# Ten gather slots instead of five, and round loops unrolled by two, in a two-layer graph network

## What is computed

```python
h = relu(layernorm(x))
# layer 0, the edge network: one message per edge
z   = concat([h[src], edge_attr]) @ W1 + b1          # 96 -> 64
m   = silu(silu(layernorm(z, g1, be1)) @ W2 + b2)    # 64 -> 64
agg = segment_sum(m, dst)
x   = x + layernorm(silu(concat([agg, h]) @ Wu + bu), gn, bn)
h = relu(layernorm(x))
# layer 1
agg = segment_sum(h[src], dst)
x   = x + (relu((h + agg) @ M1 + c1) @ M2 + c2)
```

## Time and profile before

| what | value |
|---|---|
| median of 3 runs | 7667.49 us (7646.55 to 7680.56) |
| profiled execution, whole | 7691.83 us |
| its span, first to last instruction | 7690.1 us |
| setup / edge network / update / layer 1 / last product, from | 0 / 209 / 5522 / 5870 / 7480 us |
| busy: PE, POOL, DVE, ACT | 5612.1, 4279.3, 3146.2, 2092.2 us |
| TensorE clock, mean of the span | 0.607 of full |

### The profile page before, as it was taken

The page is one execution under the profiler, slowest core; times in us unless marked ns, Lnnn a source line. Parts: engine busy times, 40 slices in busy tenths (PEclk is TensorE's granted clock), DMA queues, the critical chain, the costliest instruction groups (busy, mean ns, idle before and its releaser), DMA issues. The chain is left out here.

```text
span 7690.1 us, 119604 instructions
## 1 busy us (share of the span) xinstructions
PE 5612.1 (73%) x32337; PEld 4448.0 (58%) x32337; DVE 3146.2 (41%) x12654; ACT 2092.2 (27%) x4111; POOL 4279.3 (56%) x4223
## 2 busy tenths in 40 slices
PE   6577676776767676776767676767757888888879
PEld 5455555555555555555555555555646777777776
DVE  6333333333333333333333333333365565555651
ACT  1111111111111111111111111111135555555551
POOL 3655555555555555555555555555436666666651
PEclk9555555555555555555555555555558999999995
DMA  2111111111111111111111111111111000000001
GB/s 82 33 30 30 29 29 29 29 29 29 29 29 29 29 30 29 29 29 29 29 29 29 28 29 29 30 29 29 25 38 20 17 17 17 17 18 17 17 14 34
DMA packets 281547, 216.06 MB, mean 28 GB/s; under 512 B 152958, under 2 KB 213403, under 8 KB 280985
## 3 DMA queue, kind: packets, MB, share of 16 engines
q0 software_dynamic: 134304, 137.82, 10.1%
q1 hardware_dynamic: 147193, 77.59, 3.8%
HBM read 200.56 MB, written 14.40 MB: 28 GB/s over the span
## 5 line engine op out<-in xcount | busy, mean ns | idle before, releaser
L733 POOL DMA_INDIRECT gat<-layer_rows,idx x4025 | 4049.9, 1006 | 2929.1 <-ACT idx L791 1786.1
L770 PE MATMUL ps<-oh,edge_buffers 128*64 128x64 f32 x6250 | 874.2, 317 | 699.7 <-issue 485.1
L741 PE MATMUL ps<-w1e,edge_buffers 64*128 64x128 f32 (+1 forms) x3750 | 1136.4, 443 | 164.6 <-issue 142.7
L1497 ACT ACTIVATE node_buffers<-ps 125x800 bf16<-125x800 f32 x1152 | 947.5, 838 | 764.7 <-PE ps L1548 565.3
L770 PEld LDWEIGHTS ps<-oh,edge_buffers 128*64 128x64 f32 x6250 | 730.9, 221 | 726.2 <-issue 448.1
L741 PEld LDWEIGHTS ps<-w1e,edge_buffers 64*128 64x128 f32 (+1 forms) x3750 | 924.5, 319 | 332.6 <-issue 313.7
L749 PE MATMUL ps<-ident,edge_buffers 128*128 128x128 f32 x1875 | 563.6, 439 | 701.0 <-DVE edge_buffers L993 616.9
L922 ACT ACTIVATE edge_buffers<-ps,gcol 128x384 f32<-128x384 f32 x625 | 415.3, 665 | 1954.7 <-remote 1822.9
L797 DVE TENSOR_TENSOR cT<-cT,ps 64x64 f32 x805 | 170.8, 212 | 1881.1 <-remote 1339.0
L965 DVE TENSOR_TENSOR edge_buffers<-ps,gat 128x320 f32<-128x320 f32 x625 | 306.1, 490 | 1520.7 <-remote 1239.5
L1548 PE MATMUL ps<-node_buffers 128*128 128x200 bf16 x4608 | 646.8, 265 | 333.9 <-ACT node_buffers L1497 218.2
(11 more groups left out here) (187 smaller groups left out, 4812.6 us busy)
## 6 DMA issues: line engine op xcount, KB each, us to landing
gat<-layer_rows,idx POOLq DMA_INDIRECT x4025
edge_buffers<-in_edge_pairs SPq DMA_DIRECT2D x625, 64.0 KB
edge_buffers<-in_edge_last SPq DMA_DIRECT2D x625, 16.0 KB
node_buffers<-in_x SPq DMA_DIRECT2D x5, 625.0 KB
layer_rows<-node_buffers SPq DMA_DIRECT2D x25, 125.0 KB
residual_rows<-node_buffers SPq DMA_DIRECT2D x5, 625.0 KB
layer_rows<-node_buffers SPq DMA_DIRECT2D x5, 625.0 KB
node_buffers<-residual_rows POOLq DMA_DIRECT2D x25, 125.0 KB, 4.5
```

Of the source, the lines that this page charges most:

```text
L733: pool.indirect_dma_start(out=gat[:, j, c, :], out_offset=None, in_=table[:, :], in_offset=bass.IndirectOffsetOnAxis(ap=idx[:, j, c:c + 1] ...
L741: mm = pe.matmul(zp[j % 2][:, 2 * k * F:(2 * k + 1 + two) * F], ea[0:(1 + two) * ED, j, k * 128:(k + 1) * 128], w1e[0:(1 + two) * ED, 0:(1 ...
L770: mm = pe.matmul(to[j % 2][0:F, 0:WIN], rows_of[:, c, :], oh[:, j, c, :], start=(c == 0), stop=(c == BC - 1))
L1497: a.activation(cnt[0:TP, s, ch * 8 * T:(ch + 1) * 8 * T].rearrange("p (b k) -> p b k", b=2), built[ch % 2][0:TP, :, :], ACT.Copy).then_inc ...
```

## The change

1. **Ten slots.** Gathered rows and row numbers of the edge network get two sets of five slots each, `deep[0..1]` and `deep_idx[0..1]`, in memory that another stage uses otherwise. An even round uses set 0, an odd round set 1. There are ten completion semaphores in place of five. POOL's step for block n now waits for the row add of block n-10, and ACT writes the row numbers of block n+10 behind the squares of block n (ten sets ahead of the first step).
2. **Rounds unrolled by two.** Which set a step uses must be known when the code is written, so the loop body is now two rounds (ten steps), 60 passes; two rounds stand ahead of it on every engine, three behind it. All other buffers keep five slots.
3. **Semaphores.** To free five, the setup shares some: the two loads that DVE's offsets wait for count on one, and a few steps of one engine count on a semaphore that this engine already has. The order of the instructions stays the same.
4. Layer 1 keeps `idx` and `gat`; its counts start at 63 rounds in place of 125, since set 0 has taken the even rounds only.

```diff
+        again(XB)
+        deep = [view([128, UN, BC, F]) for _ in range(2)]
+        deep_idx = [view([128, UN, BC], i32) for _ in range(2)]
...
-                    v.wait_ge(s_dst, 16)
-                    v.wait_ge(s_head, 16)
+                    v.wait_ge(s_dst, 32)
...
-        def rounds(eng, step, lag, lead=1):
+        def rounds(eng, step, lag):
+            assert ROUNDS % 2 == 1
 
-            for j in range(lead * UN):
-                step(j // UN, j % UN)
-            with eng.Fori(lead, ROUNDS - 1) as r:
-                for j in range(UN):
-                    step(r, j)
-            for j in range(UN + lag):
-                step(ROUNDS - 1, j)
+            for j in range(2 * UN):
+                step(j // UN, j % UN, j // UN)
+            with eng.Fori(1, (ROUNDS - 3) // 2) as e:
+                for j in range(2 * UN):
+                    step(2 * e + j // UN, j % UN, j // UN)
+            for j in range(3 * UN):
+                step(ROUNDS - 3 + j // UN, j % UN, j // UN % 2)
+            for j in range(UN, UN + lag):
+                step(ROUNDS - 1, j, 0)
...
-        g_gat = [sem(f"rows_gathered{j}") for j in range(UN)]
+        g_gat = [[sem(f"l0_rows_gathered{p}_{j}") for j in range(UN)] for p in range(2)]
...
                     wait(pool, g_idx, n + 1)
 
-                    wait(pool, g_z, n - UN + 1)
+                    wait(pool, g_z, n - 2 * UN + 1)
                     wait_alone(pool, "gpsimd")
-                    gather(pool, ptab, n, j, g_gat[j])
+                    gather(pool, ptab, j, g_gat[p][j], deep[p], deep_idx[p])
...
-                        if there(n + UN):
-                            indices(a, n + UN, s).then_inc(g_idx, 1)
+                        if there(n + 2 * UN):
+                            indices(a, n + 2 * UN, s, deep_idx[p]).then_inc(g_idx, 1)
...
-                    for j in range(UN):
-                        indices(a, j, j).then_inc(g_idx, 1)
-                    rounds(a, step, 4, lead=2)
+                    for j in range(2 * UN):
+                        indices(a, j, j % UN, deep_idx[j // UN]).then_inc(g_idx, 1)
+                    rounds(a, step, 4)
...
-                        wait(v, g_gat[s], q * (16 * BC) + 16 * BC)
+                        half = q // 2 if isinstance(q, int) else q >> 1
+                        wait(v, g_gat[p][s], half * (16 * BC) + 16 * BC)
...
-                                        gat[:, s, :, :], ALU.add).then_inc(g_z, 1)
+                                        deep[p][:, s, :, :], ALU.add).then_inc(g_z, 1)
...
-        L0_ROWS = ROUNDS * 16 * BC
+        L0_ROWS = (ROUNDS + 1) // 2 * 16 * BC
```

More of the change, by code:

```diff
@@ L602, in _ @@
                 v.tensor_reduce(worst[:, 5:6], worst[:, 0:5], X, ALU.max).then_inc(s_test, 1)
[L603 to L605 removed]
+                v.wait_ge(s_tot, 3)
+                v.tensor_copy(off_i[:, :], ag[1][:, 0:NT]).then_inc(s_hk, 1)
+                v.wait_ge(s_tot, 4)
                 v.tensor_reduce(worst_row[:, :], ag[0][0:1, 0:128], X, ALU.max).then_inc(s_test, 1)
@@ L722, in _, with gather @@
                 pe.matmul(zp[0][:, 0:3 * F], ones[:, :], rows[:, 2:5, :].rearrange("o k f -> o (k f)"),
-                          start=True, stop=True).then_inc(s_bp, 1)
-                pe.wait_ge(s_deg, 3)
+                          start=True, stop=True).then_inc(s_tot, 1)
+                pe.wait_ge(s_hk, 8 + HEAD)
                 pe.matmul(ag[1][:, 0:NT], onesm[0:NT, :], carry[:, :], start=False, stop=True).then_inc(s_tot, 1)
                 pe.wait_ge(s_test, 10)
-                pe.transpose(ag[0][0:1, 0:128], worst[:, 5:6], ident[:, :]).then_inc(s_wt, 1)
-        def gather(pool, table, n, j, done):
+                pe.transpose(ag[0][0:1, 0:128], worst[:, 5:6], ident[:, :]).then_inc(s_tot, 1)
+        def gather(pool, table, j, done, to=gat, at=idx):
             for c in range(BC):
                 pool.indirect_dma_start(
-                    out=gat[:, j, c, :], out_offset=None, in_=table[:, :],
-                    in_offset=bass.IndirectOffsetOnAxis(ap=idx[:, j, c:c + 1], axis=0)).then_inc(done, 16)
+                    out=to[:, j, c, :], out_offset=None, in_=table[:, :],
+                    in_offset=bass.IndirectOffsetOnAxis(ap=at[:, j, c:c + 1], axis=0)).then_inc(done, 16)
         def edge_products(pe, j):
@@ L787, in load_edges, with indices @@
             sp.dma_start(ea[0:ED, j, (BC // 2) * 128:], of(edge_last)).then_inc(done, 16)
-        def indices(a, n, j):
-            return a.activation(idx[:, j, :], block_of(src_all, n), ACT.Copy)
+        def indices(a, n, j, to=idx):
+            return a.activation(to[:, j, :], block_of(src_all, n), ACT.Copy)
         def add_sums(v, n, j, of=ag):
@@ L850, in _, with step @@
             def _(sp):
-                def step(r, j):
+                def step(r, j, p):
                     n = r * UN + j
@@ L902, in _, with step @@
                     edge_products(pe, 0).then_inc(g_ep, 1)
-                    rounds(pe, step, 5, lead=2)
+                    rounds(pe, step, 5)
             @block.scalar
             def _(a):
-                def step(r, j):
+                def step(r, j, p):
                     _, s, n = lagged(r, j, 0)
@@ L997, in _ @@
                 with v.If(flagged(v) == 0):
-                    rounds(v, step, 6, lead=2)
+                    rounds(v, step, 6)
         def general(layer, table):
@@ L1023, in gpsimd @@
                     wait_alone(pool, "gpsimd")
-                    gather(pool, table, n, 0, x_gat)
+                    gather(pool, table, 0, x_gat)
             def scalar(a):
@@ L1467, in step @@
                     wait_alone(pool, "gpsimd")
-                    gather(pool, htab, n, j, g_gat[j])
+                    gather(pool, htab, j, g_gat[0][j])
                 def both(r):
@@ L1513, in sums @@
                     n = r * UN + j
-                    wait(pe, g_gat[j], r * (16 * BC) + L0_ROWS + 16 * BC)
+                    wait(pe, g_gat[0][j], r * (16 * BC) + L0_ROWS + 16 * BC)
                     wait(pe, k_oh, n + 1)
```

33 lines of the change are left out of this document (14 added, 19 removed).

## The result

The changed kernel took 7773.28 us (median of 4 runs, 7747.21 to 7815.74) against 7662.44 us for the kernel before beside it: a ratio of 1.0149, interval 1.0089 to 1.021. The forecast was 7685 us, +0.2%. Twelve more runs in another set gave a median of 7756.34 us against 7656.83. So the change is slower both times, by 1.4 and 1.3% in the medians, and the sign is surer than the size.

The account below looks back on a forecast made before the run. PE's signals arriving late while POOL issues gathers without a break were taken to bound the edge network. 7691.8 + 31.3 - 13.3 = 7709.8 us profiled, 24.3 above the median, so 7685 us (+0.2%); range 7550 to 7810.

Parts of the forecast that it names:

- the likeliest case: Whole kernel: start and end terms within their bounds plus the spread of runs, 7640 to 7715 us; chance 0.55.
- rival C: POOL's stream: free slots let two-block runs grow to three, 8.72 us a block, 156 us slower, 7840 us; chance 0.14.
- Rival D: DVE's loop: code fetched again each pass, 85 to 170 us slower, 7770 to 7855 us; chance 0.07.
- What bounds the kernel now: Edge network: PE's signals reach others late while POOL issues gathers without a break; 8.46 us a block.
- Ten slots, steady state: 0 us: Edge network's steady part: each row add still frees one block of gathers, so 8.46 us a block stays; bounds -270 and +156.
- Start: +31.3 us: Start of the edge network: POOL's first run grows from ten blocks to fifteen, delaying the sixth row add; bounds 0 to 31.3.
- End: -13.3 us: End of the edge network: ten blocks instead of five go at 5.81 us, not 8.46, after POOL's last gather; bounds 0 and 15.
- Loop ends: 0: Loops of each engine: 62 fewer passes over the loop's end gain nothing, being covered; 13 us gained at most.
- The longer body: 0 us: DVE's ten-step loop body: refetching its code taken as 0 us, upper bound 170 us.
- Setup: 0: Setup: shared semaphores cost nothing, since DVE waited for both loads before and shared counts come in order; 0 us.
- Rival A: POOL's runs get shorter or calmer: 8.26 us a block gives 7565 us, 8.01 gives 7415; chance 0.17.
- Rival B: Edge network becomes POOL-bound, decoupled from late signals: 6.25 us a block, 6320 us in all; chance 0.05.

Follow-up runs that it names:

- the lead of five: The changed kernel with POOL let go by the row add five blocks back and row numbers written five ahead: ratio 1.0143 to the kernel before, 7737.32 us.

## Why the prediction came out as it did

The measured 7773 us lies in the stated range of 7550 to 7810, and the likeliest case, a time within 0.5% of before's, did not occur: the loss is 111 us in the medians against the 18 of the sum. That the range held is luck. Its upper part was there for rivals C and D, and neither of them is what happened.

*What bounds the kernel now* was right for the steady part: late signals of PE's under POOL's unbroken issue, and not the gathers. Three experiments show it from three sides: fewer gathers (5.81 us a block), a POOL that stops for PE's late signals (7.80), and a chip without late signals (6.25). What the prediction could not see is that this is no fixed cost of the kernel.

*Ten slots, steady state: 0 us* was right: the lead of five costs as much as the lead of ten (1.0143), and POOL's wait is the same. The argument that a slot frees only at a row add held.

*Start: +31.3 us*: the size was near (+38.3 in the trace), the path not. POOL ran 80 gathers, not 75, since the sixth row add was not held up: it came at 281.2, inside the run. The seventh took what was foretold for the sixth, at 318.40 after 23.56 us of "remote". Where signals are on time it should not be paid; the changed kernel was not run there.

*End: -13.3 us*: -16.1 in the trace, by the mechanism given.

*Loop ends: 0* and *The longer body: 0 us* hold the step that failed. The prediction priced DVE's code alone, called SP's longer body 0, and gave PE's, ACT's and POOL's none. Rival D's sign came true to the packet, 300 more on the instruction queue, and so did its stall: DVE stands 2.97 us at the end of a pass in place of 0.38, some 156 us in all, within D's 85 to 170. What failed of D is that this reaches the end: the ratio is 1.0019, the stall hides in DVE's waits. By the Trainium skill (Runtime: NRT & Kernel Launch, "Instruction fetch mechanics") a taken branch outside the resident pages stalls; the trace agrees, with the 2.97 us. The loss came from the loops that were given no line of the sum: all five unrolled cost 2.2% (157 us in the medians), inside the bound of 170 that had been set aside for DVE, with longer pauses after runs of three blocks (8.61 us, 7.62 before). Why long loops should cost that stays open. That is nearest to rival C's place, but C said longer runs, and there are no more of them (97, 99 before). What a chance of 0.27 for slower held was the right outcome by a path that no rival named.

*Setup: 0* and the place of the slots: 0, as measured (1.0).

Rival A's pace occurred in the steady part (8.36 to 8.40 in three kernels) without a faster whole. Rival B's price per block, 6.25, is just what the undelayed chip ran at, and with five slots.

## What to carry to other kernels

Before you add slots to a pipeline, look at what ends the consumer's wait: if it is not the transfer, a deeper ring only lets the producer run further ahead. Here it did so once, at the start (80 gathers in one run in place of 50), and the start came out 38 us longer. Where PE's signals come late under a stream of indirect gathers, let the gathering engine wait for one of PE's recent signals: one wait gave 4.2 to 4.5%. Three of them cost nothing measurable where signals are on time; the version with one was not run there, nor the one with three where they are late. A stall of one engine, real and 156 us in sum, may cost nothing, so test the loops of all engines before you price one. Whether that gain exists in executions that are not recorded is not shown (below). Take the time of a kernel with such a stream on more than one chip, and don't build on a per cent that only one of them shows.

## What the runs showed of the hardware

The same program takes 7651 to 7662 us in four sets and 5950 us in a fifth, on another chip, each with little spread. The kernels traced there have the same granted clock in the edge network, 0.50, and nearly the same duration of a gather, 944 ns against 947. The difference is the delay of PE's signals while POOL gathers: none of over 0.02 us, against up to 14 us from 1000 to 5000 in the trace of before. Layer 1 differs too, 1363 against 1729 us. Whether the delay belongs to the chip or to something else that ran on it, these runs can't tell.

One rival is untested, and it is a strong one: that the recording of the profile itself holds the engines up. A gather raises its semaphore sixteen times, and of these updates over the whole execution the three traces of the quick chip have 64,376 to 64,383 of 64,400; those of the chips with late signals have 14,404 to 14,738 (16,134 and 16,768 with the added wait). Of PE's own signals 2498 of 2500 in the edge network are there on the quick chip, and 1652 of 1893 from 1000 to 5000 in the trace of before. The kernel with three gathers a block has 23,050 of 44,400, and its PE signals are on time. So many lost records go with late signals, though not one for one; whether one causes the other, or both have one cause, is not shown, and every timed execution here has its clock on record, so none is known to have run unrecorded. The figures on late signals hold for the recorded ones.

In the long run at the start, PE was given single matmuls 2.8 us apart with nothing to wait for, and DVE waited 1.2 to 3.3 us for signals of its own. The one matmul of such a step has 0.26 to 0.37 us, so what suffers is the feeding of instructions and signals, not the matmul.

A loop body whose code is fetched again each pass cost DVE 2.6 us a pass (2.97 in place of 0.38), with five packets of 8 KB, and PE's body of ten steps brought no packets (22 on the queue, as before).

A wait that makes an engine stop can raise its share: POOL went from 56% to 62% busy in the steady part.
